# Side units and the transposed row maxima behind a step's first chunk of scores instead of behind its last, in a two-block transformer kernel

## The reference, cut to what matters

```python
h = layernorm(x)
Q, K, V = (split_heads(h @ W.T + b) for W, b in ((Wq, bq), (Wk, bk), (Wv, bv)))
scores = einsum('bhqd,bhkd->bhqk', Q, K) / sqrt(16)
scores = scores + prior_lambda * gaussian_mask(2048)
attn = softmax(scores)
x = x + (merge(einsum('bhqk,bhkd->bhqd', attn, V)) @ Wo.T + bo)
```

## Time and profile before

| | us |
|---|---|
| median of 3 runs (lowest, highest) | 5565.44 (5561.8, 5568.02) |
| the profiled execution's own time | 5561.3 |
| its span | 5559.5 |
| TensorE busy in the span | 5193.5 (93%) |
| VectorE busy | 4744.1 (85%) |
| ScalarE busy | 4269.2 (77%) |
| GpSimd busy | 2185.2 (39%) |
| granted TensorE clock, mean | 0.991 |

### The profile page before, as it was taken

How to read it: one execution, slowest core, us unless ns; L and a number is a source line. 1 busy time by engine, 2 the same in 40 slices (tenths; PEclk the granted TensorE clock), 3 DMA queues, 4 the chain that set the end, 5 groups by cost and what they waited for, 6 DMA issues and landing times. The chain is left out here.

```text
span 5559.5 us, 179608 instructions
## 1 busy us (share of the span) xinstructions
PE 5193.5 (93%) x75212; PEld 3169.5 (57%) x75340; DVE 4744.1 (85%) x9925; ACT 4269.2 (77%) x8522; POOL 2185.2 (39%) x1695
## 2 busy tenths in 40 slices
PE   8889989999899998998888999999999999999999
PEld 2333333333333333333336888888887888888887
DVE  5998899998999889999967888887776888888776
ACT  3999999999999999999994777776334777777333
POOL 2011103211032110220006998995113999897222
PEclk8999999999999999999999999999999999999999
DMA  2011101111011111111103454543001454454211
GB/s 86 23 34 38 38 24 45 42 44 40 25 38 48 38 40 29 50 42 36 30 12 93 113 117 111 117 113 98 12 10 43 114 117 113 112 118 106 60 52 46
DMA packets 262970, 343.32 MB, mean 62 GB/s; under 512 B 45664, under 2 KB 165520, under 8 KB 262160
## 3 DMA queue, kind: packets, MB, share of 16 engines
q1 hardware_dynamic: 262160, 331.84, 24.0%
HBM read 104.14 MB, written 33.55 MB: 25 GB/s over the span
## 5 line engine op out<-in xcount | busy, mean ns | idle before, releaser
L659 ACT ACTIVATE a_pr<-a_w,a_expscale 128x512 f32<-128x512 f32 x4096 | 2455.6, 698 | 59.6 <-PE a_w L543 33.7
L811 DVE TENSOR_REDUCE a_mx<-a_b 128x1 f32<-128x512 f32 x2688 | 1705.3, 683 | 124.1 <-PE a_b L528 117.3
L528 PE MATMUL a_b<-a_kp,a_qp 48*32 48x512 f16 x16384 | 1424.1, 383 | 197.8 <-DVE a_mx L809 92.4
L543 PE MATMUL a_w<-a_qp,a_kp 50*32 50x512 f16 x16384 | 1459.4, 383 | 51.7 <-ACT raw L642 39.0
L565 PE MATMUL a_po<-a_pr,a_v 64*17 64x512 f32 x16384 | 1165.1, 591 | 21.5 <-ACT a_osb L692 20.6
L528 PEld LDWEIGHTS a_b<-a_kp,a_qp 48*32 48x32 f16 x16384 | 403.2, 90 | 1272.4 <-DVE a_mx L811 627.0
L809 DVE CUSTOM_DVE_ANT_0 a_junk<-a_b,a_gw 128x512 bf16<-128x512 f32 x1408 | 962.9, 684 | 105.2 <-PE a_b L528 50.1
L1709 POOL TENSOR_TENSOR l_p<-l_p,l_rc 128x512 f32<-128x512 f32 (+1 forms) x512 | 721.8, 1437 | 31.3 <-DVE l_rc L1607 31.1
L1497 ACT ACTIVATE l_p<-l_S,l_nm 128x256 f32<-128x256 f32 (+1 forms) x1024 | 470.9, 470 | 203.6 <-DVE l_nm L1599 203.6
L1351 PE MATMUL l_G<-l_wqkv,l_hT 128*128 128x512 f32 x2304 | 603.0, 406 | 9.4 <-DVE l_hT L1550 8.2
L543 PEld LDWEIGHTS a_w<-a_qp,a_kp 50*32 50x32 f16 x16384 | 413.8, 90 | 284.5 <-ACT a_pr L659 117.7
(11 more groups left out here) (258 smaller groups left out, 8855.6 us busy)
## 6 DMA issues: line engine op xcount, KB each, us to landing
l_qs<-l_qT SPq DMA_DIRECT2D x512, 128.0 KB, 2.3
l_kh<-l_kT SPq DMA_DIRECT2D x512, 128.0 KB, 2.4
l_kl<-l_kT SPq DMA_DIRECT2D x256, 128.0 KB, 2.4
a_qp<-q_parts SPq DMA_DIRECT2D x128, 128.0 KB, 2.8
a_kp<-k_parts SPq DMA_DIRECT2D x128, 128.0 KB, 3.1
l_tab<-in_rotary SPq DMA_DIRECT2D x128, 128.0 KB, 2.4
a_xc<-in_x SPq DMA_DIRECT2D x28, 512.0 KB, 3.9
q_parts<-raw SPq DMA_DIRECT2D x32, 256.0 KB, 2.3
```

The costliest lines, as they stand in the source:

```text
L528: m = eng.matmul(bk[32 * r:32 * r + 32, :], qp[s][0:DEEP, o:o + 32], kp[s][0:DEEP, c * 512:c * 512 + 512], start=True, stop=True)
L543: m = eng.matmul(bk[32 * r:32 * r + 32, :], kp[s][HALF:HALF + DEEP + 2, o:o + 32], qp[s][HALF:HALF + DEEP + 2, c * 512:c * 512 + 512], sta ...
L659: eng.activation(pr[(2 * n + c // 2) % NP][:, o:o + 512], banks[i], ACT.Exp, scale=expscale[:, :]).then_inc(s_free[i], 1)
L811: t = eng.tensor_reduce(mx[g % 2][:, qb, c:c + 1], banks[i], X, ALU.max)
```

## The change

TensorE's and ScalarE's loops do a step's unit and its rows of maxima behind chunk 0 instead of behind chunk 3, and the rows of maxima stand before the unit instead of behind it. `attention_tables` takes the column banks in the new order. The steps to which units, rows and side work belong stay as they are, and so do the loops of VectorE, GpSimd and the DMA queue.

```diff
@@ attention_tables
         for c in range(4):
             if n + LEAD < NS:
                 t.take(("rows_of", g1, qb, c), ROWS)
             if 0 <= n < NS:
                 t.take(("columns_of", n, c), COLUMNS)
-        if n in units:
-            unit(units[n], COLUMNS)
+            if c == 0 and rows_at(n):
+                t.take(("rows", rows_at(n) - 1), COLUMNS)
+            if c == 0 and n in units:
+                unit(units[n], COLUMNS)
         if n in side and side[n][0] in ("stats", "moments"):
             tick("rstd", side[n])
-        if rows_at(n):
-            t.take(("rows", rows_at(n) - 1), COLUMNS)
@@ tensor
             for c in range(4):
                 pass1(n, c)
                 pass2(n, c)
+                if c == 0 and rows_at(n):
+                    rows_T(("rows", rows_at(n) - 1))
+                if c == 0 and n in units:
+                    work[units[n][0]](units[n])
                 if c == 2:
                     pv(n - 1)
-            if n in units:
-                work[units[n][0]](units[n])
-            if rows_at(n):
-                rows_T(("rows", rows_at(n) - 1))
@@ scalar
             for c in range(4):
                 pass2(n, c)
-            if n in units and units[n][0] in work:
-                work[units[n][0]](units[n])
-            if rows_at(n):
-                rows_T(("rows", rows_at(n) - 1))
+                if c == 0 and rows_at(n):
+                    rows_T(("rows", rows_at(n) - 1))
+                if c == 0 and n in units and units[n][0] in work:
+                    work[units[n][0]](units[n])
```

## The result

The changed kernel takes 5598.39 us (median of 4 runs, 5588.64 to 5606.41) against 5565.5 before: ratio 1.0059, 95% interval 1.0038 to 1.0079. The forecast was 5591. The ten times are two groups with nothing between them: six from 5586.6 to 5592.1, and four from 5604.7 to 5607.0. The profiled execution is one of the upper group (5604.65), that of the repetition (5586.55) one of the lower.

The account below looks back on a forecast made before the run. VectorE was taken to bound plain steps, with TensorE leading by three row banks. Terms -14 + 10 - 6 - 4 + 27 + 12 + 1 gave +26 us, so 5587 profiled and 5591 us median; range 5558 to 5618.

Parts of the forecast that it names:

- Projections alone: 34 projections without other work in the step: VectorE's delay 1.90 us each against 2.36, taken as -14 us.
- With statistics or inverses: 14 projections beside this VectorE work: moved away from its cover, 3.1 us against 2.4 each, +10 us.
- Values: 24 values units, one copy each and no second stall: 1.15 us against 1.4, -6 us.
- The number of banks alone: Alternative for the repeating 1.52 us gap: if only banks mattered, moved projections keep their price, their term 0, sum +40.
- Out pieces: 24 units: lost cover of moments, and in 12 TensorE waits for GpSimd's product (L975) behind the head sum; +27 us.
- Turned and spread: 48 shorter units: spreads -6 us as ScalarE's heads copy comes sooner, turned (transposes) +2; together -4 us.
- Rows of maxima: 63 transposes behind chunk 0 take a column-ring place, so `pv` and VectorE's last chunk come later: +12 us.
- The second stall of projections: VectorE's late chunk 3 after a projection: 0.84 us before; after the move 0.75 us, from ScalarE's backlog.
- the units before the first column step: 8 projections and 2 values lie there; the first row of maxima, before the column steps, was given +1 us.
- Only the place of the gaps changes: Rival, chance 0.20, 5565 us: gaps added behind out pieces may be taken back at projections, VectorE's work being the same.
- The packed maxima come late: Rival, chance 0.15, 5603 us: GpSimd's packing is late for TensorE's earlier transpose in 11 groups, 1.3 us each, +14.
- Faster: Rival, chance 0.12, 5543 us: projections' second stall is gone; needs rows of maxima costing nothing and GpSimd's product in time.

Follow-up runs that it names:

- the repetition: The changed kernel run six more times without an edit, compared with the kernel before: 5590.0 us, ratio 1.0049; its profiled execution took 5586.55 us.
- the activation done twice: Changed kernel with ScalarE's first activation of each projection (L641) run a second time after the first ends, same result: 5628.26 us, ratio 1.0102.
- The experiment on GpSimd's order: Changed kernel with GpSimd's sum of the heads moved to the end of its step: 5565.48 us, ratio 1.0.
- the selective kernel: Changed kernel, but units go behind chunk 0 only in steps without VectorE side work, the others stay behind chunk 3: 5554.53 us, ratio 0.9979.
- the one with side work first: Changed kernel with VectorE's statistics, moments and inverses also behind its chunk 0 instead of chunk 3: 5543.5 us, ratio 0.9963.

## Why the prediction was right, point by point

- **Projections alone** (-14, measured -15.6): right by its own steps. The walk of step 346 gave 1.07 + 0.08 + 0.75, the profile has 1.13 + 0.09 + 0.67. That ScalarE's time sets the last term is shown by the activation done twice; that it does so through the exponentials and not through the bank is read from step 346, where the matmuls wait for the exponential and not for L642.
- **With statistics or inverses** (+10, measured +11.6): right, though in step 361 VectorE's gap ahead of the statistics is 0.80 us and not 1.0 to 1.2. That the lost cover is the cause is shown by moving VectorE's side work along, which brings back more than was lost.
- **Values** (-6, measured -6.6): right. The number of banks alone doesn't set the repeating gap, since the moved unit is cheaper with the same six banks. Whether a fourth row bank would shorten it too, no run here shows.
- **Out pieces** (+27, measured +33.4): the mechanism right, the size low. GpSimd's product ends at 921.53 and the wait is 1.06 us, where I had 0.9. In five of the twelve the extra is 4.4 to 4.6 instead of 3.7 us, and there TensorE's clock was at half for 3.4 us, from 8 to 9 us after the piece began; I had no term for that.
- **Turned and spread** (-4, measured +4.4): the step that failed is "Turned: ... some 0.1 each: +2". Spreads gained 5.9, as forecast. Of the 24 transposes 21 cost together what they did before, and 3 cost 4 us each. They stand in a step 2 of a group (114, 370 and 626), behind the same sum of the heads that I had found for the out pieces; I checked that wait for one kind of unit and not for the other. The experiment on GpSimd's order shows it: 16.8 to 6.0 us.
- **Rows of maxima** (+12, measured about nothing): the 34 that stand alone cost +0.6, and with the units moved the loop is 2848.4 us with the rows behind chunk 3 and 2844.3 with them behind chunk 0. The step that failed is "`pv` ... would at 1410.61 + 0.06 + 0.21 = 1410.89". I added the 0.21 us that lie between a pair and `pv` when they follow each other without a wait. When the pair's column half comes late, `pv` starts right behind it; TensorE in step 461 of the changed kernel:

```profile
1418.41 0.23 PE L573 MATMUL a_w<-a_identh,a_pk 128*32 128x128 f16 x1
...
1419.55 0.40 PE L543 MATMUL a_w<-a_qp,a_kp 50*32 50x512 f16 x4
1419.56 1.24 PE L565 MATMUL a_po<-a_pr,a_v 64*17 64x512 f32 x16
```

  The column pair does come later, as forecast, and `pv` follows in 0.01 us; that is 0.2 less (the sum as written comes to 1410.88), and VectorE's spare 0.14 us take up the rest. The earlier trace rows had shown it (1082.76, and behind it `pv`). The second stall of projections, which the walk made 0.75 and the profile 0.67, has the same 0.21 in its sum of 1.58.
- **The sum** of the loop, +26, was met at +25.8 because the rows' 11 us too much and the units before the first column step (3 too much) cancel the 15 us too little at transposes and out pieces. That is luck: the total was better than its parts.
- **The rest** of the first median's distance, 5598 against 5591, lies behind the loop's last row chunk: the clock of the last 20 steps, in two of the first four runs.
- **The rivals.** "Only the place of the gaps changes" falls by the selective kernel and by the table. "The packed maxima come late" is real where the rows move alone (+14) and is covered in the full change. Its time should read 5605 by its own sum (5591 and 14) and not 5603. "Faster" fell on both of its conditions: the backlog stays, and the product is late.

## What to carry to other kernels

Before a piece of work is moved in one engine's queue, list what ran beside it on the other engines: here a move that makes each plain unit cheaper lost 0.5%, because VectorE's side work and GpSimd's order stayed behind, and gained 0.76% once both moved along. In a queue written by hand, put what another engine waits for ahead of what waits itself: one sum in front of a product cost 25 us in the new place and nothing in the old. And walk every kind of unit past every wait, not only the one that showed it first.

## What the runs showed that I had not expected

The granted clock in the last 20 steps of the loop. There TensorE's matmuls for the rows are gone and it is busy for 36.03 of 40 us at 1.00. In 4 of the 10 runs of the changed kernel the time is 15 to 18 us longer with a mean clock of 0.983 or 0.984 instead of 0.987 to 0.989, and the one such run that was traced has the clock at 0.50 for 68 us, past the end of the loop. The kernel before has such runs too (8 of its 70, 5579.6 to 5587.0), and so have the one with GpSimd's order (5581 among 12) and the one with side work first (5559 and 5560 among 9); so the change does not make the fall; whether it makes it likelier, these numbers don't settle, nor what starts it. And inside the loop there are short falls as well: of stretches of 3.4 us at half clock between 200 and 2870 us the trace of before has one, that of the changed kernel ten, and one of 6.8 us. In the first profile all three transposes for which TensorE waits 2.2 us have one that begins in the wait, and their four matmuls take 1.09 us instead of 0.66; in the repetition two of the three do. Of the twelve out pieces with a wait of 1.06 us five have one, 8 to 9 us later, and seven have none; so a wait of that length may be followed by a fall, and these traces don't say what decides it. Where a fall came, it cost: 0.7 us at an out piece, and about 1.1 us at a projection with the doubled activation.
